# Second feed-forward product: first group in pieces, first block chunk by chunk, second block split ahead of the first residuals

## The reference, cut to what matters

```python
def quantize_w8_per(w, axis):
    amax = jnp.clip(jnp.max(jnp.abs(w), axis=axis, keepdims=True), 1e-08, None)
    scale = 127.0 / amax
    w_q = jnp.clip(jnp.round(w * scale), -128.0, 127.0) / scale
...
def quantize_a16(x):
    amax = jnp.clip(jnp.max(jnp.abs(x)), 1e-08, None)      # one maximum of the whole tensor
    scale = 32767.0 / amax
    x_q = jnp.clip(jnp.round(x * scale), -32768.0, 32767.0) / scale
...
hidden = jax.nn.gelu(x_sim @ W_in_sim + b_in, approximate=False)   # [8192, 2048]
hidden_sim = quantize_a16(hidden)
out = hidden_sim @ W_out_sim + b_out                                # [8192, 512]
...
x = _layernorm(x + out)
```

## Time and profile before

| | |
|---|---|
| median of 3 runs | 2281.64 us (2280.51 to 2283.36) |
| profiled execution, its own time | 2284.26 us |
| its span | 2282.5 us |
| TensorE busy | 2111.4 us, 93% |
| VectorE busy | 1735.8 us, 76% |
| ScalarE busy | 1082.4 us, 47% |
| GpSimd busy | 822.0 us, 36% |
| last stage, from its first instruction on hidden values | 1813.98 us to the end |
| of it, from TensorE's first matmul to its last | 1822.24 to 2270.63 us |

### The profile page before, as it was taken

The page is one execution under the profiler, slowest core; times in us unless marked ns, Lnnn a source line. Parts: engine busy times, 40 slices in busy tenths (PEclk is TensorE's granted clock), DMA queues, the critical chain, the costliest instruction groups (busy, mean ns, idle before and its releaser), DMA issues.

```text
span 2282.5 us, 32943 instructions
## 1 busy us (share of the span) xinstructions
PE 2111.4 (93%) x11904; PEld 1167.9 (51%) x11904; DVE 1735.8 (76%) x3296; ACT 1082.4 (47%) x1522; POOL 822.0 (36%) x802
## 2 busy tenths in 40 slices
PE   7999999984798998999999859999999699999997
PEld 3444444431586776777777524444444344444443
DVE  6768686865677897898898656777666488888885
ACT  1444444443444555555555224444444565555551
POOL 2122221222125555556455432222222134444442
PEclk9999999996779999999999779999999899999999
DMA  6334243457749969979975437888888656666662
GB/s 233 108 126 155 94 148 110 115 137 176 188 128 208 260 166 191 279 183 208 262 181 153 136 84 267 288 288 289 267 270 272 249 195 227 224 233 230 226 226 79
DMA packets 386626, 448.46 MB, mean 196 GB/s; under 512 B 279270, under 2 KB 279430, under 8 KB 368032
## 3 DMA queue, kind: packets, MB, share of 16 engines
q1 hardware_dynamic: 322448, 286.07, 46.0%
q0 software_dynamic: 64016, 160.28, 22.9%
HBM read 258.93 MB, written 138.73 MB: 174 GB/s over the span
## 4 chain that ended last, share of the span: by engine, by line
PE 82%; DVE 7%; issue 6%; ACT 1%; DMA 1%; POOL 1%; SPq 0%; DVEq 0%; POOLq 0%; ACTq 0%
PE ps_h L1708 19%; PE ps L1951 19%; PE ps_proj L600 10%; PE ps_o L1275 8%; PE ps_w L1304 7%; PE ps_s L620 5%; PE ps_m L1227 3%; PE ps_o L1271 3%; PE ps_m L1229 3%; PE ps_l L1253 3%; DVE rope_t L428 1%; PE ps_t L1289 1%; PE ps_l L1250 1%; DVE x_hi L411 1%; DVE stack L1099 1%
## 5 line engine op out<-in xcount | busy, mean ns | idle before, releaser
L1708 PE MATMUL ps_h<-xT,b_rows 128*128 128x512 f16 x2048 | 444.7, 381 | 13.1 <-DMA xT<-x_lo 13.1
L1951 PE MATMUL ps<-w,g_hi 128*128 128x512 f16 x1024 | 389.3, 380 | 21.1 <-DVE g_lo L1887 21.1
L1951 PE MATMUL ps<-w,g_lo 128*128 128x512 f16 x1024 | 389.1, 380 | 0.0
L1708 PEld LDWEIGHTS ps_h<-xT,b_rows 128*128 128x128 f16 x2048 | 200.9, 98 | 256.6 <-issue 16.6
L1549 ACT ACTIVATE h<-ps_h,b_rows 128x512 f32<-128x512 f32 x256 | 199.0, 777 | 241.5 <-PE ps_h L1708 241.5
L1275 PEld LDWEIGHTS ps_o<-vm,pT 128*128 128x128 f32 x2048 | 299.2, 202 | 13.0
L1099 DVE TENSOR_REDUCE stack<-ps_m 128x2 f16<-128x308 f32 x512 | 244.2, 479 | 55.3 <-PE ps_m L1229 53.6
L1275 PE MATMUL ps_o<-vm,pT 128*128 128x33 f32 x2048 | 284.8, 265 | 0.0
L1050 ACT ACTIVATE pT<-logit 128x512 f32<-128x512 f32 x320 | 199.0, 624 | 132.3 <-DVE logit L1117 131.4
L1622 DVE TENSOR_REDUCE amax_t<-h 128x1 f32<-128x2048 f32 x64 | 146.2, 2284 | 120.8 <-ACT h L1549 120.8
L1800 POOL TENSOR_TENSOR rstd<-vare,minus_half 128x1 f32<-128x1 f32 x64 | 152.3, 2380 | 208.5 <-DVE vare L1905 208.5
(11 more groups left out here) (182 smaller groups left out, 3840.1 us busy)
## 6 DMA issues: line engine op xcount, KB each, us to landing
hidden<-h POOLq DMA_DIRECT2D x64, 1024.0 KB, 6.7
hT<-hidden SPq DMA_DIRECT2D x64, 1024.0 KB, 6.2
xc<-x_cols SPq DMA_DIRECT2D x16, 1024.0 KB, 5.1
xr<-x_rows SPq DMA_DIRECT2D x16, 1024.0 KB, 5.5
x_rows<-x POOLq DMA_DIRECT2D x16, 1024.0 KB, 4.8
x1t<-x_rows SPq DMA_DIRECT2D x64, 256.0 KB, 3.8
bt_main<-bias_main SPq DMA_DIRECT2D x16, 1024.0 KB, 6.3
xres<-x_rows SPq DMA_DIRECT2D x64, 256.0 KB, 4.1
```

The source lines that it names most:

```text
L1708: mm = pe.matmul(ps_h[f % 4][:], w1[:, c, f * P:(f + 1) * P], xT[:, e, a, :, c, :], start=(a == 0 and c == 0), stop=(a == 1 and c == KC - 1))
L1951: mm = pe.matmul(ps[t][:], g[:, e, f, t * P:(t + 1) * P], w2[:, f, :], start=(f == 0 and a == 0), stop=(f == FC - 1 and a == 1))
```

## The change

It touches the last stage only, in six places.

- ScalarE and VectorE make the first group of block 0 chunk by chunk: four shifts, four scalings, four `high` and four `low` of 128x512, in place of one, four, one and one (of 128x2048, the scalings were of 128x512 already). The two engines' counts (`shifted`, `g_ready`, `hi_ready`, `lo_ready`) are three higher from there on, and all waits on them are moved by three.
- For groups 1 to 3 of block 0 VectorE runs `scale_rows(0, g)` and then `low(0, 0, g)`; before, `scale_rows(0, g + 1)` stood ahead of `low(0, 0, g)`.
- VectorE's first block: all four `scale_rows(1, t)` and `low(1, 1, t)` in turn, and then all four `residual(0, t)` and `finish(0, t)`. From `blk(1, 1)` on its order is as before.
- TensorE's block 0 runs chunk by chunk, with the four tiles inside: 8 matmuls for each chunk, and all four tiles end in the last chunk.
- SyncE issues the four group loads of block 1 first, then two rows, then group 0 of block 2, and the other rows and loads in turn as before.
- ScalarE's order of shifts and highs is the same but for the pieces.

```diff
@@ sync
-                        sp.wait_ge(shifted, 4 * n + g - 3)
+                        sp.wait_ge(shifted, 4 * n + g)
...
                 for g in range(FG):
                     load_group(1, g)
-                    load_row(0, g)
+                for t in range(4):
+                    if t == 2:
+                        load_group(2, 0)
+                    load_row(0, t)
                 for n in range(1, NBLK - 1):
                     for g in range(FG):
-                        load_group(n + 1, g)
+                        if n > 1 or g > 0:
+                            load_group(n + 1, g)
                         load_row(n, g)
@@ scalar
-                        act.wait_ge(lo_ready, k - 3)
+                        act.wait_ge(lo_ready, k)
...
-                    act.wait_ge(g_ready, k + 1)
+                    act.wait_ge(g_ready, k + 4)
...
-                shift(0, 0)
+
+                def shift_piece(c):
+                    act.activation(g32[:, 0, c], hT[:, 0, c], ACT.Identity, bias=round_c[:],
+                                   scale=h_scale[:]).then_inc(shifted, 1)
+
+                def high_piece(c):
+                    act.wait_ge(g_ready, c + 1)
+                    act.activation(g_hi[:, 0, c, :], g32[:, 0, c], ACT.Copy).then_inc(hi_ready, 1)
+
+                act.wait_ge(hT_in[0], 16)
+                shift_piece(0)
+                for c in range(4):
+                    if c < 3:
+                        shift_piece(c + 1)
+                    high_piece(c)
 
                 def blk(n, e):
                     for g in range(FG):
+                        if n == 0 and g == 0:
+                            shift(0, 1)
+                            continue
                         if g < 3:
                             shift(n, g + 1)
@@ vector
-                scale_rows(0, 0)
-                for g in range(FG):
-                    if g + 1 < FG:
-                        scale_rows(0, g + 1)
+
+                def scale_piece(c):
+                    dve.wait_ge(shifted, c + 1)
+                    dve.tensor_scalar(g32[:, 0, c, :], g32[:, 0, c, :], ROUND, row_scale[:, c:c + 1],
+                                      ALU.subtract, ALU.mult).then_inc(g_ready, 1)
+
+                def low_piece(c):
+                    dve.wait_ge(hi_ready, c + 1)
+                    dve.tensor_tensor(g_lo[:, 0, c, :], g32[:, 0, c], g_hi[:, 0, c, :], ALU.subtract).then_inc(lo_ready, 1)
+
+                scale_piece(0)
+                for c in range(4):
+                    if c < 3:
+                        scale_piece(c + 1)
+                    low_piece(c)
+                for g in range(1, FG):
+                    scale_rows(0, g)
                     low(0, 0, g)
+
+                def first_blk():
+
+                    for t in range(4):
+                        scale_rows(1, t)
+                        low(1, 1, t)
+                    for t in range(4):
+                        residual(0, t)
+                        finish(0, t)
...
-                blk(0, 0)
+                first_blk()
@@ tensor
-                                pe.wait_ge(lo_ready, 4 * n + f // 4 + 1)
+                                pe.wait_ge(lo_ready, 4 * n + f // 4 + 4)
...
-                blk(0, 0)
+                def first_blk():
+
+                    for f in range(FC):
+                        if f < 4:
+                            pe.wait_ge(lo_ready, f + 1)
+                        elif f % 4 == 0:
+                            pe.wait_ge(lo_ready, f // 4 + 4)
+                        for t in range(4):
+                            for a, g in enumerate((g_hi, g_lo)):
+                                mm = pe.matmul(ps[t][:], g[:, 0, f, t * P:(t + 1) * P], w2[:, f, :],
+                                               start=(f == 0 and a == 0), stop=(f == FC - 1 and a == 1))
+                            if f == FC - 1:
+                                mm.then_inc(o_done, 1)
+
+                first_blk()
```

More of the change, by code:

```diff
@@ L1875, in scale_rows @@
                     k = 4 * n + g
-                    dve.wait_ge(shifted, k + 1)
+                    dve.wait_ge(shifted, k + 4)
                     for c in range(4):
@@ L1883, in low @@
                     k = 4 * n + g
-                    dve.wait_ge(hi_ready, k + 1)
+                    dve.wait_ge(hi_ready, k + 4)
                     if g == 0 and not (isinstance(n, int) and n < 2):
```

## The result

The changed kernel is slower by 0.7%: 1.0072 times the time of the kernel before, 95% interval 1.0052 to 1.0092. The medians are 2294.72 us (20 runs) and 2276.16 (20 runs of the kernel before; three of them are those shown ahead of the prediction). The forecast was 13.4 us or 0.6% more, 2295.0 us. That the median lies 0.3 us from 2295.0 is luck: the forecast started from the median of three runs, 2281.64, which is 5.5 us above that of the twenty, and the two medians of twenty lie 18.6 us apart. The ratio is the sounder measure of the change: 0.7% is 16 us, its interval 12 to 21.

The account below looks back on a forecast made before the run. TensorE alone bounds the kernel from 1833.60 on, VectorE nearly a second bound. The last wait's end moves from 1888.9 to 1902.3, 13.4 us later, added to the median 2281.64: 2295.0 us, 8-in-10 range 2290.5 to 2299.5.

Parts of the forecast that it names:

- TensorE's last wait: Block 2, the second stall: TensorE waits some 4.4 us for `low(2, 3)`, until 1902.3; no later wait is added.
- The pieces and the ring: Blocks 0 and 1: pieces start TensorE 5.4 us earlier; VectorE's closed ring takes 5.84 us a group, six rings 35.0.
- The residuals without a `low` beside them: Block 0's four tiles on VectorE: `rstd` takes 0.56 instead of 2.55, so 3.04 us a tile, 12.2 for four.
- The rival with the long `rstd`: Rival, residual phase: the long `rstd` is paid there too, 8 us more, 21.4 in all, 2303.0 us; chance 0.04.
- The hold by the load: Start of block 2: the load lands at 1875.5 and holds `shift(2, 1)`, so `low(2, 0)` comes 1.5 us later.
- VectorE's free tile: Block 2, `low` to `low` free of TensorE: 6.84 us a tile, 0.07 faster than TensorE's; 6.3 if `rstd` slipped in.
- The clock: TensorE's second stall: clock taken as kept, with little conviction; a fall there would lose 2.0 us more.
- the slow restart of block 1: Block 1, after the 15 us stall: TensorE restarts at half clock, losing 2.0 us inside the slack ahead of the second stall.
- the rival with the clock's fall: Rival: TensorE's clock falls in the second stall, 15.4 us later in all, 2297.0 us; chance 0.35.

Follow-up runs that it names:

- open_ring: The changed kernel with VectorE's scaling of the next group again ahead of this group's `low` through blocks 0 and 1; stage 459.4 us (changed kernel 472.2).
- load_early: The changed kernel with the four group loads of block 2 all ahead of the third row's load in SyncE's queue; stage 467.3 us (changed kernel 472.2).
- chunks_old_order: The kernel before with the pieces and TensorE's block 0 chunk by chunk, VectorE's order as before; stage 467.6 us (kernel before 456.7).
- tile_order: The changed kernel with TensorE's block 0 tile by tile again; stage 470.8 us (changed kernel 472.2).
- pieces_alone: The kernel before with only the first group of block 0 in pieces, all orders as before; stage 458.0 us (kernel before 456.7).

## Why the prediction was right

Times in us from the first shift; the prediction's are its own, less 1813.98.

| step | predicted | measured |
|---|---|---|
| TensorE's first matmul | 2.8 | 2.9 |
| `low(0, 1)` | 10.9 | 11.0 |
| `low(1, 3)` | 45.9 | 46.1 |
| first residual | 48.1 | 48.4 |
| `scale_rows(2, 0)` | 60.3 | 60.6 |
| `low(2, 0)` | 65.4 | 66.2 |
| `low(2, 3)` | 85.9 | 85.2 |
| end of TensorE's last wait | 88.3 | 87.5 |
| from there to the last residual | 381.7 | 384.7 |

**The pieces and the ring** were right to 0.1 and 0.2 us: 5.85 a group against 5.84, from three rows of the kernel before. open_ring showed that this is the main term (12.8 of the 15.5 us).

**The residuals without a `low` beside them**: 3.04 a tile, as read from the last block. The rival with the long `rstd`, 8 us more, is out: GpSimd's `rstd` took 0.56 to 0.60 in all four tiles.

**The hold by the load** was there: ScalarE waited 16.2 us, and the shift behind it started at 1873.96. The load took 6.6 us and not the median of 6.1, which is most of the 0.8 that `low(2, 0)` was late; VectorE waited 2.17 for `g_hi` there. Put at 1.5, the hold cost 2.0: load_early takes it away and gains that.

**VectorE's free tile** was mis-sized: 6.31 us and not 6.84. In the blocks of the kernel before `low` starts 0.16 ahead of `rstd`, and `rstd` then takes 2.55. Here `low` has to wait 0.18 for `g_hi`, and `rstd` gets in first:

```profile
1884.11 0.56 POOL L1804 TENSOR_TENSOR rstd<-vare,minus_half 128x1 f32<-128x1 f32 x1 [2.56 <-DVE vare L1926]
1884.20 2.29 DVE L1908 TENSOR_TENSOR g_lo<-bt_main,g_hi 128x2048 f16<-128x2048 f32 x1 [0.18 <-ACT g_hi L1837]
1886.41 0.54 DVE L1934 TENSOR_SCALAR o<-y,mv,rstd 128x512 f32<-128x512 f32 x1
```

It takes 0.56, and `finish` follows `low` with no wait. The prediction had this as a bound (6.3 us, -1.6) and took the other end. Over three tiles it is 1.6 us.

**The clock** is the step that failed. I took it as kept through the second wait, though the sum had that wait at 4.4 us, longer than both falls that I had read, after 3.7 and 4.2 us of idling. The two reasons that I gave don't hold: the slow restart of block 1 and the load's hold were already in the 4.4, and the hold makes that wait longer, not shorter. The wait began at 83.8 us, as predicted, and lasted 3.8; the clock fell 2.8 us after TensorE's last matmul. So the rival with the clock's fall held. And its price was 3.0 where I had 2.0, because the clock came back 5.9 us after the restart and not 4.0.

So the measured 15.5 is 13.4, less 0.8 on VectorE's chain, and 3.0 for the clock (to 0.1 by rounding): the mechanism was right, and the clock's term, put at nothing, was in part made up by VectorE's quicker tiles. That the span of 2295.7 fell on the predicted 2295.9 is in part chance: the execution's earlier stages were 2.3 us shorter. So is the median's fall on 2295.0 (first section). The comparison of many runs, 0.7% or 16 us of 2276, agrees with 15.5.

## What to carry to other kernels

Before giving a nearly full engine its work in a new order, read one period of it and add up its waits. Here they were a tenth of it (0.69 of 6.93 us), and in chunks_old_order, where VectorE had to wait 10.5 us for block 0's end, the stage came out 10.9 longer. Where two engines hand a tile back and forth, starting the next tile's first step ahead of this one's last hides the other engine's step; without that its whole length is paid in each round (1.98 us in each 5.85 here). An earlier start of the engine that bounds the kernel is a gain only if its last wait moves too. And a wait of TensorE that grew by 2.0 us cost 4.9 here, since its clock fell in the longer one.

## What the runs showed of the hardware

- **The idle time at which TensorE's clock fell differed, and so did the way back.** In the changed kernel it fell 4.6 us after TensorE's last matmul in the first wait and 2.8 us in the second; in the kernel before 3.7 and 4.2 us; in open_ring 3.0 us. In tile_order it fell 0.7 us into the work behind a wait of 2.4, with two more waits shortly ahead. It stayed up through waits of 1.7 (load_early), 2.5 (open_ring) and 3.0 us (chunks_old_order, whose next matmul took 0.38). The way back took from 3.2 us of matmuls (tile_order, behind its wait of 4.4) to 5.9 (changed kernel), so behind a wait of 4.4 us the last 1768 matmuls lost 1.6 us in tile_order and 2.7 in open_ring. Waits between 2.4 and 3.8 us went either way in these runs, and a forecast for such a wait should carry both outcomes.
- **GpSimd's small power takes 0.56 us when it starts 0.09 ahead of VectorE's `low`, and 2.55 when it starts 0.16 behind it.** The second is the time until `low` has ended and 0.4 more. It holds in all of the stage: in the kernel before every `rstd` that started 0.1 to 0.3 us behind a `low` took 2.5 or 2.6, 59 of 64, and the other five 0.6. The Trainium skill ("Perfetto Trace Analysis", Optimizing Scalar/DVE Operations) tells of a read port that the two share and that some VectorE instructions hold as a lock; the trace agrees in that this `rstd` ends only after `low` has, and doesn't show the port.
- **The stages ahead of the change vary by themselves.** The first shift of the last stage came between 1797.6 us (pieces_alone) and 1822.0 (chunks_old_order), with code ahead of it that is the same in all kernels. In those two executions the matmuls of cross attention's first product ran from 527.6 to 1218.4 and from 528.4 to 1243.5 us, and the feed-forward's first product took 444 us in both. These two ran on different chips, but it isn't the chip alone: pieces_alone and tile_order ran on the same one, with first shifts at 1797.6 and 1816.1 us. Why cross attention varies so wasn't tried.
